# Graph attention, layers 2 and 3: the maximum chain of one chunk moved beside the messages of the chunk before

## The reference

```python
h = jnp.maximum(_layernorm(x, axis=-1), 0.0)
# layer 2: own loops are added to the edges
logits = leaky_relu(a_s[src] + a_d[dst], 0.2)        # 8 heads
m = segment_max(logits, dst)
e = exp(logits - m[dst]); den = segment_sum(e, dst)
out = segment_sum((e / den[dst])[:, :, None] * h[src], dst)
# layer 3: the same without own loops, with a term of each edge
alpha = leaky_relu(a_src[src] + a_dst[dst] + a_edge, 0.2)
```

## Time and profile before

| | us |
|---|---|
| median of 3 runs | 4477.2 (4475.13 to 4479.6) |
| the profiled execution | 4498.89 |
| its span, first to last instruction | 4497.1 |
| attention of layer 2, first subtraction to last | 2537.2 to 3374.6 |
| attention of layer 3, first subtraction to last | 3581.5 to 4398.1 |

### The profile page before, as it was taken

How to read it: one execution, slowest core, us unless ns; L and a number is a source line. 1 busy time by engine, 2 the same in 40 slices (tenths; PEclk the granted TensorE clock), 3 DMA queues, 4 the chain that set the end, 5 groups by cost and what they waited for, 6 DMA issues and landing times. The chain is left out here.

```text
span 4497.1 us, 59364 instructions
## 1 busy us (share of the span) xinstructions
PE 2936.8 (65%) x13774; PEld 2189.1 (49%) x13775; DVE 2316.7 (52%) x5369; ACT 1604.3 (36%) x3613; POOL 1805.9 (40%) x1951
## 2 busy tenths in 40 slices
PE   1122259997276999999983567767771576766761
PEld 0111259996134666666652345545550455544551
DVE  5000136665544778777775244444448344444447
ACT  0000014443013555555542344444441444444441
POOL 5777740000103545545530445454440344555540
PEclk9555579999598999999996566666665666666665
DMA  2000000000224555555540222222221222222220
GB/s 85 1 1 1 1 1 2 2 2 1 64 77 119 161 154 156 160 154 159 154 112 28 78 74 74 73 78 71 72 61 29 80 78 73 80 78 78 79 73 29
DMA packets 205585, 320.51 MB, mean 71 GB/s; under 512 B 101460, under 2 KB 143853, under 8 KB 205262
## 3 DMA queue, kind: packets, MB, share of 16 engines
q0 software_dynamic: 91904, 245.16, 20.3%
q1 hardware_dynamic: 113615, 74.60, 6.4%
HBM read 293.71 MB, written 27.81 MB: 71 GB/s over the span
## 5 line engine op out<-in xcount | busy, mean ns | idle before, releaser
L1500 POOL DMA_INDIRECT t_rows<-table_h,t_istage x896 | 853.8, 953 | 813.8 <-PE t_pso L1597 477.7
L1597 PE MATMUL t_pso<-t_rows,t_hot 125*125 125x272 f32 (+1 forms) x1792 | 671.4, 537 | 13.4 <-DVE t_rows L1711 9.8
L1103 POOL DMA_INDIRECT b_rows<-table_kv,b_istage x448 | 479.2, 1070 | 412.8 <-PE b_pso L1240 289.9
L1597 PEld LDWEIGHTS t_pso<-t_rows,t_hot 125*125 125x125 f32 x1792 | 449.7, 264 | 125.4 <-issue 14.9
L372 POOL DMA_INDIRECT rotation_list<-r_pstage,r_istage x400 | 393.8, 984 | 143.6 <-issue 140.3
L511 ACT COPY r_neu<-r_psn 128x384 f32<-128x384 f32 (+2 forms) x448 | 184.3, 419 | 606.5 <-remote 350.9
L1526 ACT ACTIVATE t_away_t<-t_psb,t_minus 125x500 f32<-125x500 f32 x224 | 151.5, 676 | 666.2 <-PE t_psb L1573 375.3
L1642 DVE TENSOR_TENSOR acc<-acc,t_pso 125x272 f32 (+1 forms) x448 | 192.8, 430 | 378.8 <-PE t_pso L1597 160.8
L534 PE MATMUL r_psn<-r_neu 128*128 128x128 f32 x768 | 166.0, 301 | 308.9 <-issue 200.2
L1583 PEld LDWEIGHTS t_pss<-node_scores,t_hot_t 125*125 125x125 f32 x1792 | 320.0, 267 | 69.8 <-issue 63.9
L1583 PE MATMUL t_pss<-node_scores,t_hot_t 125*125 x1792 | 330.8, 316 | 1.2 <-ACT t_hot_t L1528 0.9
(11 more groups left out here) (382 smaller groups left out, 5626.7 us busy)
## 6 DMA issues: line engine op xcount, KB each, us to landing
t_rows<-table_h,t_istage POOLq DMA_INDIRECT x896
b_attr<-in_attr_t SPq DMA_DIRECT2D x224, 62.5 KB
b_places<-targets SPq DMA_DIRECT2D x28, 488.3 KB
b_rows<-table_kv,b_istage POOLq DMA_INDIRECT x448
table_h<-d_stage SPq DMA_DIRECT2D x50, 132.8 KB
rotation_list<-r_pstage,r_istage POOLq DMA_INDIRECT x400
rotation_list<-l_pad SPq DMA_DIRECT2D x1, 4806.0 KB, 14.2
t_flag<-flags SPq DMA_DIRECT2D x56, 62.5 KB
```

The costliest lines, as they stand in the source:

```text
L1103: pool.indirect_dma_start(out=rows[:, h, s, :], out_offset=None, in_=table, in_offset=bass.IndirectOffsetOnAxis(ap=istage[:, h, s:s + 1], ...
L1500: pool.indirect_dma_start(out=rows[:, h, s, :], out_offset=None, in_=table, in_offset=bass.IndirectOffsetOnAxis(ap=istage[:, h, s:s + 1], ...
L1597: mm = pe.matmul(ps_o[b % 2][0:P, at:at + mw], hot[:, h, b * G + u, :], rows[0:P, h, b * G + u, 0:mw], start=u % PAIR == 0, stop=u % PAIR ...
```

## The change

`rows` gets four chunk buffers in place of two (`RING`). The gathers of block b of chunk c now wait for the sums of chunk c - 4. The bodies of PE, DVE and ACT are slots, one per block b of chunk c. In a slot stand the message and the sums of block b of chunk c, the add of the block before, a quarter of the maximum chain of chunk c + 1, and the target scores of block b of chunk c + 2. Two bodies before the first chunk (c = -2 and -1) start the pipeline, and the loop of the program now holds four chunks. `places` is loaded by a DMA that broadcasts it to all 125 partitions, so `spread` is gone and ACT reads the places from SBUF; both one-hot matrices are made in place. The scores have two PSUM tiles. `factor` and `most_e` share a tile and one semaphore.

Core of the diff (declarations of tiles and semaphores are cut):

```diff
-        rows = sb("rows", [ROWS, 2, RUN, RW])
-        places = sb("places", [1, 2, RUN, P], BF16)
+        rows = sb("rows", [ROWS, RING, RUN, RW])
+        places = sb("places", [P, 2, RUN * P], BF16)
...
-                        if after(c, 2):
-                            pool_wait(pool, summed, (c - 2) * B + b + 1)
+                        if not known(c, RING):
+                            pool_wait(pool, summed, (c - RING) * B + b + 1)
...
-                    sp.dma_start(places[:, h], places_of[:, bass.ds(c * RUN, RUN), :]).then_inc(loaded[h], 16)
+                    sp.dma_start(places[:, h], targets[:, bass.ds(c * (RUN * P), RUN * P)].to_broadcast([P, RUN * P])).then_inc(loaded[h], 16)
...
+                def body(c, r):
+                    chain = not known(c, -1) and not ends_at(c, CHUNKS - 1)
+                    fresh = not ends_at(c, CHUNKS - 2)
...
                     for b in range(B):
+                        if fresh:
+                            expand(c + 2, (r + 2) % RING, b, word)
+                        if chain and b == 1:
+                            pe.wait_ge(scored, c + 2)
+                            pe.transpose(peak_t, peak[:].rearrange("p s h -> p (s h)"), ident[0:P, 0:P]).then_inc(turned, 1)
+                        if chain and b == 2:
+                            pe.wait_ge(scanned, c + 2)
...
+                        if chain and b == 3:
+                            pe.wait_ge(begun, c + 2)
...
+                        if not known(c, 0):
+                            total(c, r, b)
+                    if chain:
+                        pe.wait_ge(hotset, (c + 1) * B + 1)
+                        pe.wait_ge(peaked, c + 2)
+                        pe.matmul(factor, hot[0:1, h, 0, :], fade[:, 2], start=True, stop=True)
+                        pe.transpose(most_e, most[:], ident[:]).then_inc(returned, 1)
...
+                def body(c, r):
...
+                    past = None if known(c, 1) else load_stairs(dve, g, c - 1)
+                    now = None if known(c, 0) else load_stairs(dve, g, c)
                     for b in range(B):
+                        last = block_at(c, r, b - 1)
+                        if last:
+                            add(*last, past if b == 0 else now)
+                        if not known(c, 0):
+                            if b == 0:
...
+                                dve.wait_ge(returned, c + 1)
...
+                            message(c, r, b)
+                        if chain and b == 0:
...
+                        if chain and b == 3:
```

More of the change, by code:

```diff
@@ L1465, in attend_phase @@
-        partset = [sem(f"partset{k}") for k in range(2)]
-        def halves(eng, body):
-            body(0, 0)
-            body(1, 1)
-            with eng.Fori(1, CHUNKS // 2 - 1) as i:
-                body(i * 2, 0)
-                body(i * 2 + 1, 1)
-            body(CHUNKS - 2, 0)
-            body(CHUNKS - 1, 1)
-        def after(c, n):
-            return not isinstance(c, int) or c >= n
+        gathered = [sem(f"gathered{k}") for k in range(RING * B)]
+        loaded, laned, partset = ([sem(f"{n}{k}") for k in range(2)] for n in ("loaded", "laned", "partset"))
@@ new lines, in rounds, with spans, known @@
+        def rounds(eng, body):
+            for c in range(RING):
+                body(c, c)
+            with eng.Fori(1, CHUNKS // RING - 1) as i:
+                for r in range(RING):
+                    body(i * RING + r, r)
+            for r in range(RING):
+                body(CHUNKS - RING + r, r)
+        def spans(eng, body):
+            body(-2, RING - 2)
+            body(-1, RING - 1)
+            rounds(eng, body)
+        def known(c, n):
+            return isinstance(c, int) and c < n
@@ L1565, in _ @@
+                act.wait_ge(setup, 2)
+                turn(0, 0, 0)
+                spans(act, body)
             @block.tensor
             def _(pe):
-                def spread(c, h, b):
-                    n = c * B + b
-                    if b == 0:
-                        pe.wait_ge(loaded[h], (c - h) * 8 + 16)
-                    if b or after(c, 1):
-                        pe.wait_ge(away_ts, n)
-                    pe.matmul(ps_b[0:P, 0:G * P], one[:], places[:, h, b * G:(b + 1) * G].rearrange("o u e -> o (u e)"),
-                              start=True, stop=True).then_inc(spreadset, 1)
@@ L1634, in _, with message @@
+                pe.wait_ge(setup, 2)
+                spans(pe, body)
             @block.vector
             def _(dve):
-                def add(c, b, word):
+                STEPS_OF = 9 + (2 if own else 1)
+                BEGUN = 4
+                def message(c, r, b):
+                    v = rows[0:P, r, b * G:(b + 1) * G, 0:MW].rearrange("p u (h c) -> p u h c", h=H)
+                    dve.tensor_tensor(v, v, weight[:, b * G:(b + 1) * G].unsqueeze(3).to_broadcast([P, G, H, HW]), ALU.mult).then_inc(mset, 1)
```

334 lines of the change are left out of this document (153 added, 181 removed).

## The result

| | median us | range |
|---|---|---|
| before | 4476.2 | 4460.8 to 4479.6, 4 runs |
| changed | 4644.1 | 4637.3 to 4657.2, 4 runs |

The ratio is 1.0373, 95% interval 1.0344 to 1.0402. The forecast was 4453, its range ended at 4580: wrong in sign and outside the range. The profiled execution of the changed kernel took 4657.2 us, 158.3 more than that of before (4498.9).

A forecast was written before the change was run, and what follows sets the result against it. No engine was full; VectorE and TensorE handing small pieces over in each chunk's chain bounded it. Terms -15 - 84 + 35 + 40 = -24 gave 4475 us profiled, 4453 median; range 4260 to 4580, the forecast's own 4400 to 4510.

The forecast's parts named there:

- The ring of waits: Slots of layers 2 and 3: total, add, message, next total in turn; 6.86 us a slot, border 10.2, -15 us.
- TensorE's wake-up behind a message: In each slot, from the message's end to TensorE's next total: taken as 0.1 us, an estimate.
- The clock: TensorE's totals in layers 2 and 3: one in five at the high clock, -84 us.
- The fill: Start of each layer, first scores behind the longer run of gathers: 0 to +80 us, middle +40 taken.
- The jump: Rival: jumps back of the longer loop make engines wait, 0 to +51 us on top of the forecast; chance 0.10.
- The ends of a layer: Last subtraction to last add, where the last chunk now has four slots: +17.4 us a layer, +35.
- The likeliest rival, the ring at the low clock with the full fill: Layers 2 and 3: no total at the high clock, fill of 80 us; +100, 4577 us; chance 0.28.

The follow-up runs named there:

- d1_lead: Changed kernel with VectorE's message of block b before the add of block b-1 in slots 1 to 3, run without the hold: 3544.5 us, 0.960 of before.
- e4_ring2: Changed kernel with two buffers of rows and a loop of two chunks, last four chunks written out: 4545.3 us, 1.010 of before.
- e5_first: Changed kernel with messages ahead of adds; at chunk borders last add before the subtractions, one word loaded, message 0 before rescaling: 4303.7 us, 0.958 of before.
- e9_first_pace: e5_first with a layer's first gathers paced: chunk 1 by chunk 0's chain, chunks 2 and 3 by sums two chunks before: 4269.5 us, 0.955 of before.
- e8_pause: The edit of d1_lead, plus GpSimd clearing a small tile after each second gather of a block: 4390.5 us, 0.976 of before.

## Why the prediction was wrong

Against the profiled execution it is 4657.2 where 4475 was forecast, 182 us more. That is 53 (fill) + 64 (clock) + 47 (jumps) - 3 (ends) + 20.5 (before layer 2) + 0.7 (between and behind the layers). The drawing of the waits was right. Three terms beside it failed, and each of them alone would have turned the forecast of -24 us into a loss: the clock and the fill were mis-sized, and the jumps were left out of the sum as a rival.

1. **The ring of waits: right.** Median slots of 6.84 us for 6.86, borders of 10.25 for 10.2. The chain is hidden and paid back, as drawn. Only TensorE's wake-up behind a message was misread: 0.24 us in the median, for 0.1. The 0.11 that the estimate leaned on was the distance from the factor's start to a subtraction that waited for the transpose ahead of it.
2. **The clock: wrong, 64 us.** The forecast took one total in five at the high clock, -84 us. With the jumps (47) taken out of the +12.0, the 54 periods are 35 us shorter than before, where the ring alone gave -15: some 20 us of the 84 came. The totals themselves say nearly the same: they take 3.88 us in the mean in layer 2 and 3.69 in layer 3, where those at the low clock take 3.98 and 3.87, some 30 us less for 224 of them; the other 10 of the 64 are then the ring's. The reasons against a rise that the text itself named (5.8 of 6.9 us busy, a wait of 4 us at each border) were the better evidence; the clock in the windows is 0.53 and 0.59. d1_lead shows the other side: with most of the waits taken away it stands at 0.82.
3. **The fill: a term mis-sized, 53 us.** 0 and +80 were the ends, the middle, +40, was taken, +93 came. Of these 80 are the longer run of gathers, and 13 stand behind its end: from there to the first subtraction it is 16.2 and 18.0 us, before it was 11.4 and 9.9. The case for the full price stood in the earlier trace rows. The mechanism was half right: not the ring of buffers holds the first scores but TensorE's updates during a run of gathers, and with the hold absent the term is +3 a layer.
4. **The jump: a rival with 0.10 that happened, 47 us.** VectorE stands 58.7 us at 8 jumps, 12 of which it would stand at any border. The rival had 0 to +51, for 5 jumps a layer; the loop's 5 passes have 4 jumps back, so its price of 5.1 us each would end at 41, and 5.8 came. The 25 packets that it read as all instructions brought were one of two queues; with the other it was 66, and 129 in the changed kernel. By the Trainium skill, in Runtime: NRT & Kernel Launch, Instruction fetch mechanics, a taken branch out of the two pages held forces a fetch; by that rule VectorE's 365 instructions, which can reach into a third page, can pay and 183 don't. The traces agree, e4_ring2 too. (With its waits for semaphores the trace has 385 and 193 records of VectorE in a pass.) TensorE's loop shows no stall, with 766 records in a pass, weight loads and register work counted; the same section gives TensorE a store of 2048 instructions.
5. **The ends of a layer: right**, +32.0 for +35.
6. **Probably not the change's:** 20.5 us before layer 2, the spread between executions.

The likeliest rival, the ring at the low clock with the full fill, was nearly the case that occurred. It gave 4577; what it lacked is the jumps (47) and the 20.5, while its fill, 13 short, and its clock, 20 too slow, come close to cancelling. The forecast's own range, 4400 to 4510, was too narrow for its conditions: one total in ten with a fill of 80 makes 4535, one in three with a fill of 0 makes 4357.

The old trace was itself under the hold, which goes with an old chunk of 31.0 and 30.2 us where it is 24.0 and 25.4 without. So the forecast compared a slot free of the hold with a chunk full of it. That updates were late could be seen in the old trace: the prediction quoted TensorE's wait of 5.09 us for the ends of the scans as part of the chain, and the first of these scans began 4.3 us behind the transpose that it needed (over at 2866.70), and 1.9 us behind the end of a run of gathers (2869.10):

```profile
2866.37 0.33 PE L1607 MATMUL t_pst<-con_ident,t_peak 125*128 125x125 f32 x1 [1.46 <-issue]
2868.15 0.95 POOL L1500 DMA_INDIRECT t_rows<-table_h,t_istage  x1 [0.30 <-issue]
2871.01 0.42 DVE L1670 TENSOR_TENSOR_SCAN t_head<-t_flag,t_pst 128x125 f32<-128x125 bf16 x1 [2.61 <-DMA table_h<-d_stage]
```

That the lateness can be absent, no view of the old trace could give. Without the hold the wait is 1.63, in the kernel before:

```profile
2167.47 0.27 PE L1609 MATMUL t_pst<-con_ident,t_head 128*1 128x128 f32 x1 [1.63 <-DVE t_tail L1671]
```

I took what stood in the earlier trace rows for a rule of the fill alone. Where no update is held, the same change costs 9.7%.

## What to carry to other kernels

When work of one engine is split into slots, draw the ring of waits of a slot: message, sum, add. If the consumer's add stands ahead of the next message, both engines work by turns; the same calls in the other order made the kernel 2.5% (with the hold) and 4% (without) faster than before, in place of 3.7% and 9.7% slower. Count the instructions of the longest loop body after unrolling more chunks into it, and compare both queues of instructions before and after. And when an engine starts long after its producer has finished, look at what a third engine issues meanwhile before calling it the buffers.

## What had not been expected of the hardware

- While GpSimd issues indirect gathers without a pause, TensorE's semaphore updates can be late: up to 7.0 us in runs of 8 (e5_first), 22 and 42 us in longer ones (e9_first_pace), where they came some 22 us apart. ScalarE's and VectorE's aren't. A run of 4 (5 us) did no harm in the slots of the changed kernel, a pause of 0.3 to 0.5 us no good in e8_pause. It was there in 13 traces and absent in 7, and with it the kernel before takes 4476 to 4497 us, without it 3694 to 3700. Why, and whether it is GpSimd's issue or the data's landing that delays, stays open.
- A jump back in VectorE's loop costs 0.5 to 0.6 us with two chunks in the loop (e4_ring2), and 5.8 us in the mean with four, about twice the instructions (the changed kernel).
